# The first spline's stage of a graph network on one core: hat functions moved to ScalarE, two buffers of each tile, outer products issued a block ahead

## The reference

```python
pos = pseudo * (KS - 1)                                  # KS = 5, pseudo: [E, 3] in [0, 1]
i0 = jnp.clip(jnp.floor(pos), 0, KS - 2).astype(jnp.int32)
frac = pos - i0
combos = jnp.asarray(_COMBOS)                            # 8 corners
basis = jnp.prod(jnp.where(combos[None] == 1, frac[:, None, :], 1.0 - frac[:, None, :]), axis=-1)
idx = jnp.sum((i0[:, None, :] + combos[None]) * jnp.asarray(_STRIDES)[None, None, :], axis=-1)
...
z = jnp.einsum('ni,kio->nko', x, W).reshape(N * K, Fout)  # K = 125, Fin = 1, Fout = 64 here
gathered = z[col[:, None] * K + idx]
msg = jnp.einsum('es,eso->eo', basis, gathered)
out = jax.ops.segment_sum(msg, row, num_segments=N)
```

## Time and profile before

| | |
|---|---|
| median of three runs | 7320.52 us (7303.47 to 7342.39) |
| the profiled execution, its own time | 7357.94 us |
| its span, first to last instruction | 7355.8 us |
| mean granted TensorE clock over the span | 0.855 |
| PE busy | 4635.6 us (63%) |
| DVE busy | 4183.0 us (57%) |
| ACT busy | 1654.2 us (22%) |
| POOL busy | 4443.2 us (60%) |

### The profile page before, as it was taken

The page is one execution under the profiler, slowest core; times in us unless marked ns, Lnnn a source line. Parts: engine busy times, 40 slices in busy tenths (PEclk is TensorE's granted clock), DMA queues, the critical chain, the costliest instruction groups (busy, mean ns, idle before and its releaser), DMA issues. The chain is left out here.

```text
span 7355.8 us, 95916 instructions
## 1 busy us (share of the span) xinstructions
PE 4635.6 (63%) x31067; PEld 3408.4 (46%) x31067; DVE 4183.0 (57%) x9381; ACT 1654.2 (22%) x2811; POOL 4443.2 (60%) x4319
## 2 busy tenths in 40 slices
PE   5444442876638888888554667999992444544433
PEld 4444442655536666665443434555552333333322
DVE  7555553769946666666442316777773445444433
ACT  1111120117824444444231000000000222222211
POOL 2777776000057777777433256777764777777763
PEclk9999999569979999999776788999996777777766
DMA  4222221013332222224866581111111111111385
GB/s 73 78 71 78 71 78 26 21 36 151 160 76 54 52 53 53 54 52 49 37 30 180 195 270 39 38 37 37 37 34 23 19 18 18 19 19 18 17 14 14
DMA packets 388448, 441.47 MB, mean 60 GB/s; under 512 B 241139, under 2 KB 312320, under 8 KB 387981
## 3 DMA queue, kind: packets, MB, share of 16 engines
q0 software_dynamic: 137696, 130.26, 18.3%
q1 hardware_dynamic: 191113, 286.63, 12.4%
q10 hardware_dynamic: 59568, 23.69, 1.4%
HBM read 358.46 MB, written 82.34 MB: 60 GB/s over the span
## 5 line engine op out<-in xcount | busy, mean ns | idle before, releaser
L951 POOL DMA_INDIRECT at_far<-att_table,at_rec x1184 | 1227.7, 1037 | 886.0 <-DMA at_rec<-rec_r 400.9
L1524 POOL DMA_INDIRECT p_far<-table,p_rec x1184 | 1242.1, 1049 | 488.2 <-issue 359.9
L2162 PE MATMUL g_l_ps_sum<-g_l_row,g_l_of 128*128 128x392 f32 x3224 | 1062.9, 493 | 19.4 <-DVE g_l_of L2113 19.4
L534 POOL DMA_INDIRECT rec_r<-so_r_rec,so_r_place x806 | 835.0, 1036 | 245.5 <-issue 245.5
L2084 POOL DMA_INDIRECT g_l_got<-table,g_l_index x806 | 811.1, 1006 | 245.5 <-issue 228.4
L2162 PEld LDWEIGHTS g_l_ps_sum<-g_l_row,g_l_of 128*128 128x128 f32 x3224 | 613.2, 190 | 469.7 <-DVE g_l_of L2113 20.6
L1422 PE MATMUL p_ps_outer<-p_spread,p_basis 128*25 128x40 f32 (+1 forms) x4736 | 758.9, 341 | 77.9 <-DVE p_spread L1367 53.1
L1422 PEld LDWEIGHTS p_ps_outer<-p_spread,p_basis 128*25 128x25 f32 (+1 forms) x4736 | 636.0, 183 | 207.6 <-issue 94.5
L1422 PE MATMUL at_bank<-p_spread,p_basis 64*125 64x256 f32 x4736 | 629.3, 418 | 107.1 <-ACT p_outer L1477 107.1
L2096 DVE TENSOR_SCALAR g_l_row<-g_l_iota,edge_row 128x784 f32<-128x784 f32 x806 | 500.3, 693 | 222.2 <-PE g_l_ps_sum L2162 222.0
L489 PE MATMUL so_r_look<-so_r_table,so_r_lo_t 128*128 128x26 f32 x1612 | 425.0, 433 | 310.8 <-DVE so_r_table L433 310.8
(11 more groups left out here) (457 smaller groups left out, 6201.2 us busy)
## 6 DMA issues: line engine op xcount, KB each, us to landing
adjacent<-ad_by_chunk SPq DMA_DIRECT2D x74, 800.0 KB, 3.3
so_r_row<-pad_src SPq DMA_DIRECT2D x62, 832.0 KB, 6.2
g_l_counts<-adjacent SPq DMA_DIRECT2D x60, 800.0 KB, 6.9
g_l1d_counts<-adjacent SPq DMA_DIRECT2D x59, 800.0 KB, 7.1
so_r_low<-pad_lo_src SPq DMA_DIRECT2D x62, 416.0 KB, 4.7
at_far<-att_table,at_rec POOLq DMA_INDIRECT x1184
p_far<-table,p_rec POOLq DMA_INDIRECT x1184
rec_r<-so_r_rec,so_r_place POOLq DMA_INDIRECT x806, 2.1
```

Source lines behind the costliest of these rows:

```text
L534: pool.indirect_dma_start(out=o.rec[:, :], out_offset=bass.IndirectOffsetOnAxis(ap=place[b][:, j:j + 1], axis=0), in_=rec[b][:, j, :], in_ ...
L951: pool.indirect_dma_start(out=far[b][:, t, :], out_offset=None, in_=g.att_table[:, :], in_offset=bass.IndirectOffsetOnAxis(ap=rec[b][:, t, ...
L1524: pool.indirect_dma_start(out=sl.far[b][:, t, :], out_offset=None, in_=table[:, :], in_offset=bass.IndirectOffsetOnAxis(ap=sl.rec[b][:, t, ...
L2162: last = nc.tensor.matmul(ps_sum[k][:], of4[b][:, j, :, :].rearrange("p k f -> p (k f)"), row1[b][:, j, k * COLS:(k + 1) * COLS], start=Fa ...
```

## The change

`stage_spline_ones` no longer uses `Spline` but has its own code. Nothing else changes but its call in `layers`; the attention's stage and the third spline's stage keep the class.

- The hats are made on ScalarE: eight activations of 96 numbers for each block (five rising sides into `hat`, three falling sides into `down`), with scale 4 or -4 and a bias from small tiles of constants. VectorE keeps one operation of them, the smaller of the two sides for the three inner hats (288 numbers).
- `basis` is made in one operation of 800 numbers instead of two of 400.
- `rec`, `keep`, `hat`, `down`, `basis`, `spread`, `outer`, `run` and the banks of the outer products have two buffers each. `carry` is gone: the scan takes its start from the last column of the other `run`.
- `keep` is loaded by SyncE, a block ahead, no longer by ScalarE.
- TensorE's order is now outer products of block n, turn of block n-2, product through the weights of block n-1. VectorE scans block n-2 behind the spread of block n. ScalarE makes the hats of block n+1, copies the outer products of block n, then stores the rows of block n-2.
- The first four blocks and the last are written out; the rest are a loop over pairs of blocks.

```diff
+            @block.scalar
+            def _(act):
+                def make_hats(n, b, turn):
+                    act.wait_ge(rec_in[b], turn * 16 + 16)
+                    if early(n) >= 2:
+                        act.wait_ge(spreads, n - 1)
+                    at = rec[b][:, :, 1:4].bitcast(F32)
+                    up, to = (lambda k: hat[b][:, :, :, k]), (lambda k: down[b][:, :, :, k])
+                    nc.scalar.activation(up(0), at, ACT.Relu, bias=offs[:, 0:1], scale=-4.0)
+                    nc.scalar.mul(up(1), at, 4.0)
+                    for k in (2, 3, 4):
+                        nc.scalar.activation(up(k), at, ACT.Relu, bias=offs[:, k:k + 1], scale=4.0)
+                    nc.scalar.activation(to(0), at, ACT.Relu, bias=offs2[:, 0:1], scale=-4.0)
+                    nc.scalar.activation(to(1), at, ACT.Relu, bias=offs2[:, 1:2], scale=-4.0)
+                    nc.scalar.activation(to(2), at, ACT.Identity, bias=offs2[:, 2:3], scale=-4.0).then_inc(hats, 1)
+                def copy_products(n, b):
+                    act.wait_ge(products, n + 1)
+                    if early(n) >= 2:
+                        act.wait_ge(made, n - 1)
...
+                def one(n, b, turn):
+                    if early(n) < last_block:
+                        make_hats(n + 1, 1 - b, turn + b)
+                    copy_products(n, b)
+                    if early(n) >= 2:
+                        store_rows(n - 2)
...
+                def scan(n, b, turn):
+                    dve.wait_ge(made, n + 1)
+                    dve.wait_ge(keep_in[b], turn * 16 + 16)
+                    if early(n) >= 2:
+                        dve.wait_ge(turned, n - 1)
+                    if early(n) >= 1:
+                        dve.wait_ge(scanned, n)
+                    nc.vector.tensor_tensor_scan(run[b][:], keep[b][:], ps_out[:], run[1 - b][:, V - 1:V], ALU.mult, ALU.add).then_inc(scanned, 1)
+                def one(n, b, turn):
+                    dve.wait_ge(hats, n + 1)
+                    ch.put(nc.vector.tensor_scalar(there[:], rec[b][:, :, 0], float(N), None, ALU.is_lt))
+                    ch.step(nc.vector.tensor_tensor(hat[b][:, :, :, 1:4], hat[b][:, :, :, 1:4], down[b][:], ALU.min))
+                    ch.put(nc.vector.tensor_mul(third[:], hat[b][:, :, 2, :], there[:].unsqueeze(2).to_broadcast([P, TB, J])))
+                    if early(n) >= 2:
+                        dve.wait_ge(products, n - 1)
...
-                with pe.Fori(1, o.blocks) as n:
-                    sl.outer_products(pe, n)
-                    sl.turn(pe, n - 1)
-                    sl.through_weights(pe, n)
...
+                def outer_products(n, b):
+                    pe.wait_ge(spreads, n + 1)
+                    if early(n) >= 2:
+                        pe.wait_ge(outers, n - 1)
...
+                def through_weights(n, b):
+                    pe.wait_ge(outers, n + 1)
+                    if early(n) >= 1:
+                        pe.wait_ge(scanned, n)
...
+                def one(n, b, turn):
+                    outer_products(n, b)
+                    if early(n) >= 2:
+                        turn_rows(n - 2, b)
+                    if early(n) >= 1:
+                        through_weights(n - 1, 1 - b)
```

More of the change, by code:

```diff
@@ L1607, in _, with load_keep @@
             def _(sp):
[L1608 to L1621 removed]
+                def load_keep(n, b):
+                    sp.dma_start(keep[b][:], keep_v[:, bass.ds(n * V, V)].to_broadcast([OUT, V])).then_inc(keep_in[b], 16)
@@ L1636, in _ @@
-                sl.points(dve, ch, 0, 0, 0, first=True)
-                sl.spread(dve, 0, 0, range(sl.XS))
-                following(1, 1, 0)
-                with dve.Fori(1, o.pairs) as i:
-                    ch.restart()
-                    for b in two:
-                        following(i * 2 + b, b, i)
-                ch.restart()
-                if o.odd:
-                    following(o.blocks - 1, 0, o.pairs)
-                sl.scan(dve, ch, o.blocks - 1)
+                all_blocks(dve, one, ch.restart)
```

147 lines of the change are left out of this document (110 added, 37 removed).

## The result

| | before | changed |
|---|---|---|
| median | 7324.27 us (4 runs, 7303.47 to 7342.39) | 7203.06 us (4 runs, 7199.32 to 7204.58) |
| profiled execution, its own time | 7357.94 us | 7204.02 us |
| its span; mean granted clock | 7355.8 us; 0.855 | 7201.8 us; 0.868 |
| PE, DVE, ACT, POOL busy | 4635.6, 4183.0, 1654.2, 4443.2 us | 4555.3, 4068.6, 1735.2, 4447.1 us |

The ratio is 0.983, with a 95% interval of 0.9816 to 0.9844: 121 us faster. The prediction was 7250 us with a range of 7212 to 7292.

The account below looks back on a forecast made before the run. The stage was taken as bound by TensorE at the half clock. Its 37 blocks were summed as 33 x 7.0 + 4 x 9.3 = 268 us instead of 339.5, gain 71 us, giving 7250 us, range 7212 to 7292.

Parts of the forecast that it names:

- The pause goes: TensorE's wait for ScalarE's copies before the product through the weights goes: 1.01 to 1.1 us, 37 times, 39.7 us.
- VectorE: VectorE's remaining work a block: `basis` 0.99 us, the minimum 0.46, in sum 4.2 us instead of 7.0.
- ScalarE: Eight added activations on ScalarE, 0.16 to 0.31 us each, taken at 0.31: 2.5 us a block.
- The chain: From outer run n through copies, store, hats and VectorE to outer run n+2: 8.1 us of 9.9, 1.8 us slack.
- rival 2: Stage's clock full throughout as PE no longer pauses: 5.1 us a block, 189 us, gain 150, 7170; chance 0.04.
- SyncE: Record loads behind the scan's wait stay hidden: there by 4.8 us, wanted at 6.2; otherwise up to 1 us a block.
- Start and end: 0.7 us gained before the stage's first outer product, about 1 us waiting for a scan at its end; together nothing.
- 33 x 7.0 + 4 x 9.3 = 268 us: The stage's 37 blocks: 33 partly at full clock, 7.0 us each, 4 at half clock, 9.3 each, instead of 339.5 us.
- mixed block: A block with TensorE's clock full for only part of it: 6.6 us at best, taken at 7.0.
- forecast's own range: Stage's blocks from all at 6.6 us (244 us, gain 95, 7225) to an even mixture with half-clock blocks (7281).

Follow-up runs that it names:

- double_through: Changed kernel with the five products through the weights made twice, sums unchanged; settled block 10.52 us against the changed kernel's 5.64.
- hats_sooner: Changed kernel with ScalarE making hats of block n+2 right after the copies, before the store, and SyncE loading records before the older `keep`; settled block 5.92 us.
- four_more: Changed kernel with the last four outer products of each block made again into the same place; settled block 6.83 us, total 7238.13 us.
- sixteen_more: Changed kernel with the last sixteen outer products of each block made again into the same place; settled block 6.84 us, total 7239.72 us.
- eight_more: Changed kernel with the last eight outer products of each block made again into the same place; settled block 6.16 us, total 7228.24 us.
- interleaved: Changed kernel, hats and record loads earlier, with block n-2's products through the weights put singly between block n's outer products; settled block 12.51 us.

## Why the prediction was wrong in size

- **The pause goes.** Right: 37 waits, 39.7 us, are gone without a successor at that place.
- **VectorE.** Right: `basis` 983 ns (0.99 predicted), the minimum 451 ns (0.46), 143.23 / 37 = 3.9 us a block for 4.2. (The 4.4 us for scan and preparation are 4.3 by their own terms, 0.1 + 0.74 + 3.45; nothing hangs on it.)
- **ScalarE.** An activation takes 0.36 to 0.47 us, outside my 0.16 to 0.31; the estimate of 0.38 by the Trainium skill ("ScalarE: Activation LUTs", rules for kernel authors) is nearer. But they overlap: three of L1682 take 0.98 us in the timeline, and each starts some 0.27 us behind the last, so the eight take 2.2 us for 2.5 predicted. The sum was right by the wrong number, as a mean duration is no price in a pipelined row.
- **The chain.** Right: rival 2 had put it at 5.1 us a block at the full clock, and two full blocks are 5.45 + 5.14, 5.3 on average, with waits of 0.4 to 0.5 us for `spread`. PE's own work it had too low, 4.7 us for 4.97: a full outer run takes 2.41 us, not the 2.1 worked out from the 33 ns of one 1 us window.
- **SyncE.** Nearly right: ScalarE waits 15.1 us for records, of them 7.7 at the start; none of it stands as a wait of PE of its own. That it would show at the full clock I had not priced.
- **Start and end.** 1.6 us gained at the start (0.7 predicted), two waits of 0.9 us at the end (1 predicted).
- **The step that failed: "33 x 7.0 + 4 x 9.3 = 268 us".** I read in the earlier trace rows that the clock rises in an outer run "and falls again within the block", and carried this over: every block mixed at best, at 6.6 to 7.0 us. The mixed block itself was priced at 7.0 in the sum and 6.6 at best, and takes 6.50 us in the trace, 11 such blocks in all. But two of three blocks are not mixed, they are wholly at the full clock, 5.0 to 5.8 us, a kind that the trace before doesn't have. 213.5 us came in place of 268, 54.5 less, and that is the miss: 50 us between a gain of 121 and one of 71.
- **What stood in its place.** In the kernel before the full clock never lasted from one outer run to the end of the next; with the pause gone it mostly does, and a settled block takes 5.64 us at 0.907, where the sum had 7.0. The runs show the cause as far as this: put the pause back and the full blocks vanish (8.53 us, 0.700), put a third of it back and they vanish too (8.01, 0.639); make the hats on VectorE again and one is left in the 26 settled blocks (7.00, 0.745). They don't show that it had to come so: four more outer products a block, 0.3 us of work, would have made it 6.83 us, and the forecast nearly right.
- **The rivals.** Rival 2 named the mechanism and was given 0.04, with 189 us for the 213.5 measured; 7170 for 7203. I held one stretch at 0.50 with PE 90% busy against it. That stretch speaks against "busy, hence full clock" and double_through bears this out, at 0.65 with PE busy throughout. By the Trainium skill ("TensorE: Matmul & The Clock Gate", why this matters for your kernels) rival 2 would have been the forecast; it would have come nearer, though its reason fails in this case's own runs. As I read it now, which is argued and not shown, the two kernels differ in a feedback: a faster clock shortens the block, and what the clock does in a shorter block was outside the rows. That asks for a wide range between 5.1 and 7.0 us a block, a sum from 189 to 268, 7170 to 7250, and not for a forecast's own range that ends at 6.6.

## What to carry to other kernels

When a stage's time hangs on TensorE's granted clock, price its blocks at each level and at each mixture, the one that is wholly fast included even if no block of the trace is, and spread the range over them: here the same work took 5.64 to 8.01 us a block by a wait of 0.4 us. Judge a change there by time x clock beside the time: hats_sooner cut the first by 5%, lost it in the clock, and its total is that of the changed kernel. And small edits of such a loop (an order, a few more products) are worth trying one by one, since they are cheap and no single theory forecast their outcomes.

## What was not expected of the hardware

- TensorE that is busy without a gap had a mean granted clock of 0.65 (double_through), 0.75 (four_more), 0.82 (hats_sooner), 0.88 (sixteen_more), 0.89 (eight_more). The clock also falls in the midst of an outer run, 0.6 us after its start at 1353.78.
- In this stage each of 320 rises came during an unbroken run of products over 128 rows (25 x 40) or within 1 us of its end; with the run cut into pieces by products over 25 rows, and 1.97 us of idle time a block, 325 us passed at 0.500 (interleaved). Other stages of the same kernel have rises in other products, over 64 rows for instance (L1422, 64 x 256, 24 rises in the profile of the changed kernel), so this is no rule for all products.
- Less work made a block no shorter: 5.83 us with two of five products through the weights (one execution), 5.64 with all.
- More outer products had no order: +1.20, +0.53 and +1.21 us a block for four, eight and sixteen, for 0.3, 0.6 and 1.2 us of work.
- Executions of 7.2 and of 9.2 ms in total of the same kernel had the same settled block, 5.64 us at 0.907.

What decides between the patterns stays open, and so does why the pause costs more ahead of the outer products (9.72 us) than ahead of the product through the weights (8.53).
